# Attention over gathered edges: row subtractions from GpSimd to VectorE, gathers issued before landings are announced, blanking writes moved to the dense stages

## The reference

```
q, k, v = n @ Wq + bq, n @ Wk + bk, n @ Wv + bv      # 4 heads of 512
alpha   = (q[dst] . k[src]) / sqrt(512)               # per edge and head
attn    = softmax of alpha over the edges of one dst
agg     = segment_sum(attn * v[src], dst)
x_attn  = agg + n @ Wskip + bskip
h       = x_attn @ Wlin + blin + x_attn[:, :512]
x       = x + gamma * layernorm(h) + beta
```

## Time and profile before

| | |
|---|---|
| median of 3 runs | 2274.02 us (2271.47 to 2278.88) |
| profiled execution, its own time | 2281.38 us |
| its span, first to last instruction | 2279.3 us |
| TensorE busy | 1859.0 us (82%) |
| VectorE busy | 1349.0 us (59%) |
| ScalarE busy | 906.4 us (40%) |
| GpSimd busy | 771.1 us (34%) |
| mean granted TensorE clock | 0.909 of full speed |
| DMA | 224.10 MB, mean 98 GB/s |

### The profile page before, as it was taken

One profiled execution on the slowest core, in us unless ns is written; L12 is line 12 of the kernel. 1 busy time (PEld: TensorE's weight loads), 2 busy tenths in 40 slices (PEclk: granted clock), 3 DMA queues, 4 the chain that ended last, 5 costly groups with the idle time before them and its releaser, 6 DMA issues. The chain is left out here.

```text
span 2279.3 us, 32000 instructions
## 1 busy us (share of the span) xinstructions
PE 1859.0 (82%) x10998; PEld 1562.7 (69%) x10998; DVE 1349.0 (59%) x3024; ACT 906.4 (40%) x1712; POOL 771.1 (34%) x777
## 2 busy tenths in 40 slices
PE   8997798586776776766877589999999989889686
PEld 6765697365655555555656469989878888778575
DVE  6252112556567566666775535556557868768766
ACT  4331244344434334434434212333335555555521
POOL 0000013456445445545643001111314444444244
PEclk9999898798898888988978799999998999999889
DMA  6843345344443433343421230201420111120442
GB/s 223 254 132 111 137 135 140 119 128 125 123 120 104 118 113 111 118 120 96 106 71 49 88 97 1 83 29 37 150 70 22 33 41 27 28 55 9 166 144 98
DMA packets 178678, 224.10 MB, mean 98 GB/s; under 512 B 88753, under 2 KB 119984, under 8 KB 177010
## 3 DMA queue, kind: packets, MB, share of 16 engines
q1 hardware_dynamic: 112633, 140.69, 20.2%
q0 software_dynamic: 49760, 62.92, 9.7%
q10 hardware_dynamic: 16136, 18.64, 2.3%
HBM read 177.87 MB, written 65.38 MB: 107 GB/s over the span
## 5 line engine op out<-in xcount | busy, mean ns | idle before, releaser
L1005 POOL DMA_INDIRECT edge_rows<-xn_store,edge_index x200 | 259.8, 1299 | 378.5 <-issue 138.6
L1387 PE MATMUL psum<-ident,edge_rows 125*128 125x125 f32 x800 | 149.3, 320 | 145.7 <-DVE edge_xt_lo L1225 84.8
L2472 POOL TENSOR_TENSOR mprob<-mprob,mrden 125x1250 f32<-125x1250 f32 x80 | 181.6, 2271 | 245.5 <-DVE mrden L2578 245.4
L1387 PEld LDWEIGHTS psum<-ident,edge_rows 125*128 125x128 f32 x800 | 115.6, 168 | 184.5 <-DVE edge_xt_lo L1225 96.1
L1106 ACT ACTIVATE edge_xt_hi<-psum 128x500 fp32r<-128x500 f32 x200 | 116.3, 588 | 242.7 <-PE psum L1387 242.5
L1225 DVE TENSOR_TENSOR edge_xt_lo<-psum,edge_xt_hi 128x500 fp32r<-128x500 f32 x200 | 132.8, 674 | 120.2 <-ACT edge_xt_hi L1106 118.7
L2501 ACT ACTIVATE mprob<-psum,mbias 125x1250 f32<-125x1250 f32 x80 | 104.3, 1304 | 172.3 <-DVE mbias L2587 172.3
L2585 DVE TENSOR_REDUCE mmin<-psum 125x1 f32<-125x512 f32 (+1 forms) x240 | 127.1, 584 | 49.4 <-PE psum L2744 48.8
L2762 PE MATMUL psum<-ident,mprob 125*125 125x125 f32 x800 | 120.6, 297 | 33.0 <-DVE ptm_lo L2592 26.2
L2762 PEld LDWEIGHTS psum<-ident,mprob 125*125 125x125 f32 x800 | 103.1, 196 | 49.9 <-DVE ptm_lo L2592 35.8
L1030 POOL TENSOR_TENSOR edge_rows_lo<-edge_rows,edge_rows_hi 125x512 fp32r<-125x512 f32 x100 | 126.7, 1295 | 24.5 <-ACT edge_rows_hi L1122 23.5
(11 more groups left out here) (527 smaller groups left out, 5585.5 us busy)
## 6 DMA issues: line engine op xcount, KB each, us to landing
slots_in<-blank_rows SPq DMA_DIRECT2D x40, 513.0 KB
t_store<-t_out ACTq DMA_DIRECT2D x80, 125.0 KB, 1.8
q_chunk<-q_store SPq DMA_DIRECT2D x40, 250.0 KB, 5.4
edge_attr<-in_attr SPq DMA_DIRECT2D x50, 125.0 KB
t_raw<-t_store SPq DMA_DIRECT2D x10, 600.0 KB, 9.6
moe_xg<-slots_in SPq DMA_DIRECT2D x17, 256.5 KB, 3.7
raw_WvT<-in_WvT SPq DMA_DIRECT2D x4, 1024.0 KB, 7.0
raw_WskipT<-in_WskipT SPq DMA_DIRECT2D x4, 1024.0 KB, 7.4
```

The source lines that it names most:

```text
L1005: nc.gpsimd.indirect_dma_start(xe[t % 4][:, s, :], None, g.xn_store, bass.IndirectOffsetOnAxis(ap=index[t % 4][:, s, 0:1], axis=0)).then_i ...
L1387: last = nc.tensor.transpose(x_bank(n)[:, s * P:(s + 1) * P], xe[t % 4][:, s, k * 128:(k + 1) * 128], g.ident[0:P, 0:P])
L2472: nc.gpsimd.tensor_tensor(prob[:, n % 4, :], prob[:, n % 4, :], rden[:, n % 4:n % 4 + 1].broadcast_to([P, N]), ALU.mult).then_inc(p_ready, 1)
```

## The change

Three edits in the loop, and one that moves work out of it. (1) `rest` is gone; VectorE's `rows_lo` subtracts all four groups in one instruction and waits for both halves of ScalarE's high part. (2) On GpSimd, `gather(t+3)` stands ahead of `landed(t+2)`. (3) On ScalarE, `t_tops(t+1)` stands behind the exponentials. (4) The 41 blanking writes are issued in `dense_stages`, paced by `u_done` over chunks 1 to 3 of the first FFN.

```diff
@@ gpsimd, loop over the windows
-            def rest(t):
-                pool.wait_ge(xe_top, 2 * t + 2)
-                pool.wait_ge(x_done, KT * t + KT)
-                for s in (2, 3):
-                    last = nc.gpsimd.tensor_tensor(xe_lo[t % 4][:, s, :], xe[t % 4][:, s, :], f32(xe_hi[t % 2][:, s, :]),
-                                                   ALU.subtract)
-                last.then_inc(xe_pool, 1)
...
                 for t in range(WINDOWS):
-                    rest(t)
                     if t + 1 < WINDOWS:
                         offsets(t + 1)
                         others(t + 1)
+                    if t + 3 < WINDOWS:
+                        gather(t + 3)
                     if t + 2 < WINDOWS:
                         landed(t + 2, turn)
-                    if t + 3 < WINDOWS:
-                        gather(t + 3)
@@ scalar
                         for k in range(KT):
                             x_hi(t + 1, k)
-                        t_tops(t + 1)
                     if now:
                         exponentials(t)
                     if more:
+                        t_tops(t + 1)
                         attr_hi(t + 1)
@@ vector
             def rows_lo(t):
-                dve.wait_ge(xe_top, 2 * t + 1)
+                dve.wait_ge(xe_top, 2 * t + 2)
                 dve.wait_ge(x_done, KT * t + KT)
-                nc.vector.tensor_tensor(xe_lo[t % 4][:, 0:2, :], xe[t % 4][:, 0:2, :], f32(xe_hi[t % 2][:, 0:2, :]),
-                                        ALU.subtract).then_inc(xe_dve, 1)
+                nc.vector.tensor_tensor(xe_lo[t % 4][:], xe[t % 4][:], f32(xe_hi[t % 2][:]), ALU.subtract).then_inc(xe_dve, 1)
@@ tensor, values(t)
                 pe.wait_ge(xe_dve, t + 1)
-                pe.wait_ge(xe_pool, t + 1)
@@ sync, loop over the windows
-                    if t < 41:
-                        blanks(2 * t, 2 if t < 40 else 1)
...
-                sp.wait_ge(blank_out, 16 * 41)
@@ sync, dense_stages (BLANKS = 40, LAST = 4, NE = 4, KT = 4)
             sp.dma_start(w1_raw[0][:], w1_src[0]).then_inc(w1_in[0], 16)
+            for i in range(BLANKS):
+                sp.wait_ge(u_done, UNITS + KT * (i * (LAST - 1) * NE // BLANKS))
+                blanks(2 * i, 2)
+            blanks(2 * BLANKS, 1)
             sp.wait_ge(u_done, UNITS * LAST + KT)
...
             load_q(sp, g, 0, 1)
+            sp.wait_ge(blank_out, 16 * (BLANKS + 1))
```

More of the change, by code:

```diff
@@ L826, in graph_attention @@
     p_done, p_top, p_low, r_ready = (loop_sem(n) for n in ("p_done", "p_top", "p_low", "r_ready"))
-    xe_top, xe_dve, xe_pool = (loop_sem(n) for n in ("xe_top", "xe_dve", "xe_pool"))
+    xe_top, xe_dve = (loop_sem(n) for n in ("xe_top", "xe_dve"))
     y_done, y_out, yt_done, yt_top, yt_low = (loop_sem(n) for n in ("y_done", "y_out", "yt_done", "yt_top", "yt_low"))
     o_done, o_added, base_in, base_out = (loop_sem(n) for n in ("o_done", "o_added", "base_in", "base_out"))
-    xin_in, xin_ready, xin_used, blank_out = (loop_sem(n) for n in ("xin_in", "xin_ready", "xin_used", "blank_out"))
+    xin_in, xin_ready, xin_used = (loop_sem(n) for n in ("xin_in", "xin_ready", "xin_used"))
     dve_inner, pool_inner = loop_sem("dve_inner"), loop_sem("pool_inner")
@@ L920, in t_load @@
                              ).then_inc(t_in[q], 16)
[L922 to L925, removed]
             def pair(ap, c):
@@ L1484 @@
 SLOTS = -(-N // 128) * 128
+BLANKS = NE * SLOTS // 256
 ROW = D + 1
@@ L1589, in dense_stages @@
     bias_made, bias_in = sem("moe_bias_made"), sem("moe_bias_in")
+    blank_out = sem("slots_blank_out")
     turned = g.turned.again()
@@ L1641, in second_in, with blanks @@
                 sp.dma_start(raw[e % 2][:], fc2_src[e]).then_inc(raw_in[e % 2], 16)
+            def blanks(first, n):
+                dst = g.slots_in[128 * first:128 * (first + n), :].rearrange("(i p) d -> i p d", p=128)
+                src = g.blank.rearrange("(i p) d -> i p d", i=1).broadcast_to([n, 128, D + 1])
+                sp.dma_start(dst, src).then_inc(blank_out, 16)
             sp.dma_start(fc1_raw[1][:], fc1_src[1]).then_inc(fc1_in[1], 16)
```

## The result

The changed kernel takes 2542.57 us (median of 4 runs, 2530.77 to 2547.14) against 2276.45 for the kernel before on the same chip: a ratio of 1.1154, interval 1.1094 to 1.1214. The forecast was 2231. It is 266 us slower, and far outside the range.

What follows compares the result with a forecast made beforehand. No engine bounds the kernel: the loop is a ring of short steps on all engines. Its gaps were to fall from 845.9 to 802.7 us; 43 us off the 2274.0 median gives 2231, own range 2195 to 2260, overall 2178 to 2285.

Steps and rivals of the forecast that it cites:

- Part 3: Blanking writes moved from loop to dense stage: some 21 MB in 73 us, cost 0, up to 20 us if slower.
- the slower rivals: Loop: announcement waits for gather issue, 2380 us, chance 0.07; landings stay late or clock low, 2274 to 2290, chance 0.15.
- Part 1: Loop's row subtractions all on VectorE: GpSimd stalls go, x_lo comes 2.4 us later a turn, bounds +1.07 to +2.4.
- 79.5 us of stalls on the one-column operation: Loop, VectorE's L1239: stalls behind GpSimd's row subtractions in 35 of 50 turns, 79.5 us, expected to go.
- Part 2: GpSimd's loop order, gather ahead of landing announcement: cost 0, gathers get time to land, TensorE's 60.1 us wait goes.
- ordinary turn of 17 us: Loop: sign that the announcement waits for the gather issue, a turn of 17.2 us; that rival's chance 0.07.
- the 60.1 us: Loop: TensorE's wait for GpSimd's announcement that gathered rows have landed, expected to vanish with gathers issued ahead.
- The landing of 4.3 us: Late in the loop, without blanking: time from last gather instruction to announcement, 4.3 us, against 6.5 us available.
- The price of the longer L1260 for the gathers: Loop: VectorE's longer subtraction holds up GpSimd's gather issue by up to 1.1 us, off the path.
- Part 4: ScalarE's loop order, t_tops behind the exponentials: 0, bounds -0.5 to +0.5 us a turn.
- The sum for the loop, 802.7: Loop's 49 gaps: 389 + 120 + 136.8 + 118.4 + 38.5 = 802.7 us, 43 less than 845.9.
- eight finishing turns: Eight loop turns with other finishing steps: each loses 3 us of stall and gains 2.4, 136.8 from 140.3 us.

Runs made afterwards that it cites:

- before_moved_sixteen: The kernel before, with only the blanking writes moved to the dense stage and cut into 16 stretches outermost: 2210.47 us, ratio 0.9694.
- rows_alone: before_moved_sixteen plus the whole row subtraction on VectorE, behind both halves of ScalarE's copy: 2261.47 us, ratio 0.9938 to the kernel before.
- the four loops: Four kernels with the changed kernel's loop, differing only behind it; their loops took 805, 810, 815 and 820 us.
- rows_in_halves: rows_alone with VectorE's row subtraction in two instructions, the first released by ScalarE's first half: 2151.91 us, ratio 0.9448 to the kernel before.

## Why the prediction was wrong, by its own steps

- **Part 3, the blanking: the step that failed.** It took 289 GB/s for writes that run at 55. The figure came from dividing the loop's 110 GB/s by its share of 0.38, which assumes that all sixteen engines share the work; these writes had two. The term was 0, with a bound of 20 us; it is about 300, since 21 MB take 390 us in a stretch of 90, and SyncE's queue holds the weights behind them. The kernel's line `(i p) d -> i p d` with two tiles, and an issue of up to 13.0 us for one that takes 0.65 in the median, were both there to be read. None of the slower rivals had a case for it: they looked for the slow side in GpSimd's order and in late landings.
- **Part 1: right in the turn, wrong in what it removes.** 2.29 us for the instruction, 2.4 us of TensorE waiting for x_lo, the stalls nearly gone. But taking away 79.5 us of stalls on the one-column operation gives less than that: in a loop with timely gathers TensorE's wait for the exponentials falls by 43 us, its wait for x_lo grows by 78, and TensorE's busy time for the same matmuls grows by 20 (594.7 us in before_moved_sixteen, 615.0 in rows_alone). Net it costs 49 us.
- **Part 2: the mechanism right, the gain put in the wrong place.** No ordinary turn of 17 us; the announcement costs TensorE at most 1.3 us at a time. The queue of eight instructions that the Trainium skill gives GpSimd ("Advanced Engine Details and Errata", "Engine Queue Depths") agrees with that too. But the 60.1 us do not belong to the order: they go when the writes are spread or moved, and stay (79.0) with the new order and the writes as they were. The order alone is then worth 10 us at most, hardly clear of noise. The landing of 4.3 us was an upper bound and no measurement: that announcement, at 1104.8, stands right behind the mask, whose instruction on GpSimd starts at 1104.73. The price of the longer L1260 for the gathers is as named: an indirect DMA's issue takes 1570 ns on average and not 1299, 4 x 0.27 = 1.1 us a turn, off the path.
- **Part 4:** forecast as 0; 28 us without Part 1. Beside Part 1 it was run only together with Part 2, and the two make no difference there.
- **The sum for the loop, 802.7, was right by luck: its errors cancel.** Measured one by one from 845.9: spreading or moving the writes -65, the row subtraction +49, the two orders about -17 (the mean of the four loops, 812.6, less rows_alone's 830.1, little more than the 15 us by which equal loops differ). The forecast had the gain in Parts 1 and 2. Its eight finishing turns are also added up wrong by a little: 3 us less and 2.4 more in each leave 135.5 from 140.3, not 136.8.

## What to carry to other kernels

Before a transfer is moved or counted as free, read the outermost axis of both its sides. With two there, these writes ran at the share of two of the sixteen DMA engines, were slow by themselves, and made the gathers of another queue land late. The sign in a profile is a DMA share that stands at a few whole sixteenths (0.13, 0.25), or an issue that lasts as long as the transfer. And a stall is worth what the engine that sets the turn waits for it, not the stalled engine's own sum; a step that is lengthened on the path should start with the half whose input is there first.

## What the runs showed of the hardware

- A DRAM to DRAM write gave 27 GB/s per DMA engine in large packets (55 on two, 109 on four), 235 at a share of 0.66 in 16 stretches, and 147 GB/s at a share of 0.93 in packets of about 2 KB.
- Writes on SyncE's queue that were cut for two engines delayed gathers issued through GpSimd's own queue: from 400 to 1100 us, TensorE's wait for their announcement was 57.5 us with the writes cut in two and 1.6 with sixteen stretches, at 116 and 126 GB/s in all.
- In rows_alone 17 of 23 idle stretches of 2.4 us on TensorE were followed by slower matmuls, up to 0.76 us for 0.47 (the level of 1.2 GHz for part of the turn); in rows_in_halves none of 21 stretches of 1.3 us was. Taking 1.07 us out of a turn therefore gave 86 us in 49 turns, not 50.
